# When the last two expert weight pairs are loaded and split: a fused attention and mixture-of-experts kernel

## The reference

```python
x = x + attention(xn) + ffn(xn)
# attention: 16 query heads, 4 key/value heads; semantic and rotary (geo) scores of width 32 each;
#   all keys but the last 128 are averaged in blocks of 64 -> 14 block keys + 128 local keys
# ffn: 16 experts (256 -> 224 gated by silu -> 256), the best 4 of each token, weights renormalised
```

## Time and profile before

| | |
|---|---|
| median of 3 runs | 429.58 us (429.53 to 430.78) |
| the profiled execution's own time | 429.53 us |
| its span in the trace | 427.7 us |
| TensorE (PE) busy | 368.4 us, 86% |
| DVE, ACT, POOL busy | 256.4, 185.9, 242.9 us |
| mean granted TensorE clock | 0.948 of full speed |

### The profile page before, as it was taken

One profiled execution on the slowest core, in us unless ns is written; L12 is line 12 of the kernel. 1 busy time (PEld: TensorE's weight loads), 2 busy tenths in 40 slices (PEclk: granted clock), 3 DMA queues, 4 the chain that ended last, 5 costly groups with the idle time before them and its releaser, 6 DMA issues.

```text
span 427.7 us, 8599 instructions
## 1 busy us (share of the span) xinstructions
PE 368.4 (86%) x2259; PEld 309.5 (72%) x2260; DVE 256.4 (60%) x816; ACT 185.9 (43%) x537; POOL 242.9 (57%) x211
## 2 busy tenths in 40 slices
PE   0599996889989997995469999999999999998970
PEld 0483475678856775674259999999999999988860
DVE  4888235799347999999156555555555555544430
ACT  1541246455312652136165555555555555445430
POOL 3501556565653568936088665765655755546573
PEclk9999998989999999699569999999999999999995
DMA  7990212221249640179324766766864766647443
GB/s 252 364 296 28 75 67 84 76 75 68 70 134 314 188 151 24 49 212 250 115 70 80 118 102 112 114 107 102 127 104 88 124 106 107 104 80 118 49 53 46
DMA packets 49016, 51.36 MB, mean 120 GB/s; under 512 B 5473, under 2 KB 46049, under 8 KB 48993
## 3 DMA queue, kind: packets, MB, share of 16 engines
q0 software_dynamic: 14640, 19.34, 27.1%
q1 hardware_dynamic: 34352, 31.74, 26.3%
HBM read 29.63 MB, written 21.43 MB: 119 GB/s over the span
## 4 chain that ended last, share of the span: by engine, by line
PE 62%; DVE 12%; DMA 9%; issue 7%; ACT 5%; POOLq 2%; POOL 1%; SPq 1%; another core or an unknown queue 0%; DVEq 0%; ACTq 0%
PE bank L1234 52%; DMA out_rows<-y,idx 7%; PE bank L1593 3%; PE bank L1611 3%; DMA x_all<-in_L_attn_x 1%; POOL out_rows L640 1%; DVE l L1054 1%; POOLq L633 1%; PE bank L1358 1%; DVE lmax L1057 1%; DVE pr L1180 1%; ACT x_all L662 1%; PE bank L1246 1%; ACT wgu_hi L713 1%; ACT lex L730 1%
## 5 line engine op out<-in xcount | busy, mean ns | idle before, releaser
L640 POOL DMA_INDIRECT out_rows<-y,idx x79 | 122.0, 1545 | 73.6 <-ACT y L824 34.2
L618 POOL DMA_INDIRECT xn_by_expert<-x_all,slot_i x64 | 66.1, 1033 | 20.4 <-issue 15.7
L1234 PE MATMUL bank<-wgu_hi,xh 128*128 x158 | 65.7, 416 | 6.2 <-DVE xl L1213 3.8
L1218 DVE SCALAR_TENSOR_TENSOR act<-bank,xg,sg 128x224 f32<-128x224 f32 x79 | 35.5, 450 | 55.9 <-ACT sg L811 52.4
L1213 DVE TENSOR_TENSOR xl<-bank,xh 128x256 fp32r<-128x256 f32 x79 | 33.5, 424 | 44.4 <-ACT xh L802 37.6
L1234 PE MATMUL bank<-wgu_lo,xh 128*128 x158 | 59.1, 374 | 0.0
L1234 PE MATMUL bank<-wgu_hi,xl 128*128 x158 | 58.7, 372 | 0.0
L811 ACT ACTIVATE sg<-bank 128x224 f32<-128x224 f32 x79 | 28.3, 358 | 57.8 <-PE bank L1234 52.9
L1234 PE MATMUL bank<-wdn_hi,ah 112*128 x158 | 51.6, 326 | 1.0 <-DVE al L1226 0.6
L824 ACT COPY y<-bank 128x256 f32<-128x256 f32 x79 | 29.5, 374 | 39.9 <-PE bank L1234 18.0
L1234 PE MATMUL bank<-wdn_hi,al 112*128 x158 | 44.7, 283 | 0.0
(11 more groups left out here) (218 smaller groups left out, 768.9 us busy)
## 6 DMA issues: line engine op xcount, KB each, us to landing
xg<-xn_by_expert SPq DMA_DIRECT2D x79, 129.0 KB
wgu<-in_L_ffn_gate_proj SPq DMA_DIRECT2D x16, 224.0 KB, 6.4
wgu<-in_L_ffn_up_proj SPq DMA_DIRECT2D x16, 224.0 KB, 6.6
wdn<-in_L_ffn_down_proj SPq DMA_DIRECT2D x16, 224.0 KB, 7.1
x_all<-in_L_attn_x SPq DMA_DIRECT2D x8, 256.0 KB, 4.8
xr<-in_L_attn_x SPq DMA_DIRECT2D x16, 128.0 KB, 4.9
out_rows<-xr SPq DMA_DIRECT2D x16, 128.0 KB
out_rows<-y,idx POOLq DMA_INDIRECT x79
```

The costliest lines, as they stand in the source:

```text
L618: gp.indirect_dma_start(xs_d, bass.IndirectOffsetOnAxis(slot_i[:, z, r:r + 1], 0), x_all[:, z, :], None).then_inc(xs_in[q], DMA)
L640: gp.indirect_dma_start(out_rows, bass.IndirectOffsetOnAxis(idx[r % RING][:, 0:1], 0), ysb[r % 4][:, :], None, compute_op=ALU.add).then_in ...
L1218: nc.vector.scalar_tensor_tensor(av[t.par][:, :], bank[2 + t.par][:, I:2 * I], xg[t.slot][:, D + 1:D + 2], sg[t.par][:, :], ALU.mult, ALU. ...
L1234: return nc.tensor.matmul(o, lhsT, rhs, start=start, stop=stop)
```

## The change

`SPLITS` moves the high parts of experts 10 and 11 from attention tile 6 to the list at the start of the expert pipeline, which now has six experts. SP loads only pair 3 (experts 10, 11) at i = 4 ahead of the store; pair 4 (12, 13) goes behind the store of tile 4 and the residual load of tile 6, and pair 5 (14, 15) behind the store of tile 5. The number and size of all transfers and casts stay the same.

```diff
-        SPLITS = ((), (4, 5), (6, 7), (8, 9), (), (), (10, 11), (12, 13, 14, 15))
+        SPLITS = ((), (4, 5), (6, 7), (8, 9), (), (), (), (10, 11, 12, 13, 14, 15))
@@ the loop of SP over the attention tiles
                 if i == REMOTE - 3:
                     for q in range(GROUPS):
                         sp.wait_ge(xs_in[q], K * GT * DMA)
-                    for n in range(3, (E - EARLY) // 2):
-                        load_pair(n)
+                    load_pair(3)
                 store_sum(i)
                 if i + 2 < REMOTE:
                     load_residual(i + 2)
+                if i >= REMOTE - 3 and i < REMOTE - 1:
+                    load_pair(i)
```

## The result

| | before | after |
|---|---|---|
| median of 17 runs each | 428.82 us | 432.8 us |
| lowest and highest | 426.37 and 430.78 | 431.01 and 436.35 |
| profiled execution, its span | 429.53, 427.7 us | 431.69, 429.8 us |

The ratio is 1.009, with a 95% interval of 1.0067 to 1.0111: the changed kernel is 3.9 us slower. The forecast was 428.8 us, 0.7 faster, in a range of 426.9 to 430.9; both the sign and the range were wrong.

What follows compares the result with a forecast made beforehand. PE was taken to bound the expert stage (busy 94.95 of 95 us), so its start moves all that follows; -3.8 (earlier splits) + 2.7 (two more) + 0.4 (holds) = -0.7 from 429.53 gave 428.8 us, range 426.9 to 430.9.

Steps and rivals of the forecast that it cites:

- Attention without POOL beside it: Attention tile 6: without POOL's splits of 10 and 11, the last add comes 3.0 or 4.7 us earlier.
- The first task tiles: Start of the expert stage: first tile lands at 207.5 at the earliest, ACT's splits start 3.8 us earlier.
- A first tile behind 209: Start of the expert stage: the first task tile landing after 209 us would show the forecast wrong.
- Two more casts ahead of the silu: ACT before the first silu: six splits instead of four, all of the two more counts, +2.7 us.
- POOL's late start: POOL's first scatter comes 2.95 us later but is caught up; price 0, bounds 0 and 2.95 us.
- Rival 3: Expert stage: POOL's late start is not made up, +0.3 to +0.8, 430.1 us; chance 0.11 together with rival 4.
- Held index operations: DVE in the first tasks: two to three more index operations held beside POOL's splits, +0.4 us, bounds 0 and 3.5.
- The total worked out by that reading, 428.4 us: DVE's holds end with the POOL instruction in progress and fit the gaps, hold term 0: 429.53 - 1.1 = 428.4 us.
- Rival 1: Seam after attention: full clock, no queueing of first tiles, holds fit the gaps, -2.0, 427.3 us; chance 0.25.
- Rival 2: First tasks: three further index operations each held through two POOL instructions, clock low, +2.4, 431.9 us; chance 0.12.
- Rival 4: Load queue: pair 5 at 220 GB/s ends 1.5 us later, +0.8, 430.3 us; chance 0.11 together with rival 3.

Runs made afterwards that it cites:

- e3: The changed kernel (after), with pair 5 issued behind the first two task tiles instead of behind the store of tile 5; 1.0006 of before.
- e13: e5, with only three of six high parts made ahead of the first silu and the others in the next three steps; 1.0085 of before.
- e11: e10, with POOL starting its low parts only when the high part of expert 12 is there; 1.0013 of before, 4.7 us slower than e10.
- e10: Before, with pair 5 behind two task tiles, POOL's low parts of 10, 11 after attention, one-input index operation, three of four high parts ahead of silu; 0.9903 of before.
- e12: e5, with DVE making the low parts of experts 10 to 12 ahead of the first silu; 0.9971 of before, 3.7 us faster than e5.
- e5: After, with the index operation reading one SBUF tile and a per-partition scalar instead of two tiles; 1.0058 of before.
- e4: After, with DVE making the low parts of experts 10 and 11 ahead of the first silu, POOL those of 12 to 15; 1.0115 of before.
- e6: e3, with DVE making the low parts of experts 10, 11 and 12 ahead of the first silu, POOL the rest; 1.0064 of before.

## Why the prediction was wrong

*Attention without POOL beside it: right.* 4.3 us were gained (3.0 to 4.7 expected), at full clock, and the residual was no longer waited for.

*The first task tiles: the first step that failed, and wrong by its own numbers.* "The first task tile ... lands behind them at 207.5 at the earliest", and so 3.8 us less for the start of the casts. Measured: the tile landed at 209.8 (211.0 without the lead), and the term was 0.9 us, not 3.8. A first tile behind 209 was one of the prediction's own signs of being wrong. The prediction had one pair with a store through in 5.5 us, where 1.64 MB at its own 259 GB/s are 6.3, the next pair by 206.3 and the last store by 207. Its own figures added up in one go, 3.28 MB for two pairs and two stores and 0.26 for two tiles at 259 GB/s from 195.5, give 209.2; the queues carried 13.50 us x 274 GB/s = 3.7 MB from 196.0 to 209.5. That start, 197.2 without the lead, is 1.7 us later than the 195.5 of the prediction and makes up nearly all of the rest. With 0.9 in place of 3.8 the sum would have been +2.2 us, so this term is 2.9 of the 4.6 us between the forecast (-0.7) and the result (+3.9). e3 puts its price at 3.6 us of the 3.9 (about 2 to 5).

*Two more casts ahead of the silu: right in length, not always in what it bears on.* Six took 8.16 us, the silu followed at once, 2.7 us more. But e13 took half of the six away and won nothing. The prediction passed the silu's date on to the end; what passes on is the later of the tasks' and the scatters' dates.

*POOL's late start: the second step that failed.* "Price taken: 0." Through the late casts POOL's first scatter came 4.6 us later by the trace (5.9 without the lead) instead of 2.95. The prediction set scatter 0 against y of task 4 and found it nearly hidden, 0.3 us into ACT's idle time; with the tiles late the scatter landed near 237.9, and y of task 4 was another 0.8 us late for it. What it had right is that the scatters catch up: without the lead they are 5.9 us late at task 0, 3.3 at task 7 and 2.4, as late as the tasks themselves, at task 21. What it had wrong is the place of the price. It is the one wait at task 4, which holds PE up by a time that it does not win back, where the tasks are otherwise early. e11 against e10 puts 4.7 us on 6.6 us of lateness. e12 against e5 puts 3.7 us on it in the changed kernel without holds; of e5's 2.5 us behind e12 after their first tasks (3.9 to 4.0 at the end, 1.5 at task 0) 1.0 comes by task 6, most of the rest behind task 54, where y waits for scatters again and again. In after itself the holds had made tasks 3 and 4 so late that only those 0.8 us were left, and they were won back. Rival 3 named the late start and got a few per cent, with +0.6 instead of +3.9 for a price. The 3.6 us of e3 and the 3.7 of e12 are not to be added: the late tiles act in part through the late scatter, and both remove it in part.

*Held index operations: right in kind and nearly in size.* Five instead of three, as expected; those of tasks 3 and 4 took 1.29 and 2.30 us, and y of task 3 is 1.2 us later against task 0 for them. Against this the first three were shorter (1.68, 0.62 and 0.62 instead of 2.26, 1.51 and 1.82), and y of task 0 follows the first silu by 6.94 us instead of 7.60. Together that is about 0.6 where 0.4 was taken. The Trainium skill ("SBUF — State Buffer", "Who interferes with whom") gives the shared port for a whole instruction to whoever issues first, which the prediction read as a hold that ends with the POOL instruction in progress; the measurement decides: in after one hold of five ended with a second POOL instruction (230.95 to 233.25), in e4 one lasted to the end of a third. The total worked out by that reading, 428.4 us, was out by 4.4 us, for the two reasons above.

*Rivals 1, 2 and 4.* Rival 1 fell with the queue. Rival 2 (holds through two POOL instructions) had the right sign for another cause; e4 and e6 show that such holds are real. Rival 4 named the right place (late data) and gave it 1.5 us of lateness, +0.8 in all, where it was 2.9.

*Still open.* How much of the 3.9 us falls to holds alone (e5's interval overlaps that of after); why a hold sometimes lets several POOL instructions pass; and what happens behind task 50, where the profiles of the kernels change their distance from before by -0.5 to +2.4 us, in no order with scatter 0. The two profiled executions differ by 2.2 us, 3.4 with the lead of 1.24 taken off, which lies within the interval of the 3.9 (2.9 to 4.8).

## What to carry to other kernels

When a wait on one queue is shortened, add up all bytes that stand in the queue ahead of the next transfer, in one sum from the first idle moment, and compare it with the date at which that transfer is now wanted. Where an engine has a second duty behind the first (here POOL's scatters behind its low parts), follow the first item of the second duty to who waits for it through a ring of buffers: the chain may catch up by itself, but the one wait that it causes stops the engine that bounds the stage, and that engine has no idle time to win it back. And a small instruction that can be held by another engine's long ones should be rewritten in the form that is not.

## What the runs showed of the hardware that was not expected

- A DVE operation on two SBUF tiles beside a train of POOL subtractions was held for 4.95 us (e4) and 4.50 us (e6), past the ends of three POOL instructions or more; the same work with one tile and a per-partition scalar took 0.20 us beside POOL instructions of the same kind and size (e5).
- One 129 KB tile load took 5.0 us from issue to landing with pair 5 still moving ahead of it in SP's queue (after), 2.0 to 2.1 without (before, e3).
- In after PE's clock was still granted in full (2.4 GHz) at 205.0 us, 3.6 us after its last work at 201.4, and had fallen to half (1.2 GHz) by 205.5; at the end of attention a gap of 1.66 us in PE's work cost no clock.
